# 16-head attention: ScalarE's blocks move from one PSUM ring to another

## The reference

```python
Q = (hs @ q_w + q_b).reshape(B, S, H, HD).transpose(0, 2, 1, 3)      # H = 16 heads
K = (hs @ k_w + k_b).reshape(B, S, H, KPH).transpose(0, 2, 1, 3)     # KPH = 4
V = (hs @ v_w + v_b).reshape(B, S, H, KPH).transpose(0, 2, 1, 3)
scores = einsum('bhsk,bhtk->bhst', Q[..., :KPH], K) / sqrt(KPH)
attn = softmax(scores, axis=-1)
ao = einsum('bhst,bhtv->bhsv', attn, V)       # 16 heads x 4 values, padded to 128
mla_out = ao @ o_w + o_b
```

## Time and profile before

| | |
|---|---|
| median of 3 runs | 1462.62 us (1462.22 to 1463.78) |
| the profiled execution | 1462.41 us |
| its span, which all positions below refer to | 1460.3 us |
| granted TensorE clock, mean | 0.943 of full speed |
| busy in the span: PE, VectorE, ScalarE, GpSimd | 1284.1, 1015.8, 931.7, 510.8 us |

### The profile page before, as it was taken

How to read it: one execution, slowest core, us unless ns; L and a number is a source line. 1 busy time by engine, 2 the same in 40 slices (tenths; PEclk the granted TensorE clock), 3 DMA queues, 4 the chain that set the end, 5 groups by cost and what they waited for, 6 DMA issues and landing times.

```text
span 1460.3 us, 17118 instructions
## 1 busy us (share of the span) xinstructions
PE 1284.1 (88%) x6134; PEld 693.6 (47%) x6134; DVE 1015.8 (70%) x1814; ACT 931.7 (64%) x1200; POOL 510.8 (35%) x358
## 2 busy tenths in 40 slices
PE   6999998999899999666878877899989999986666
PEld 3444453445344544331222222477756767763344
DVE  7788858885888578165776778356548676668895
ACT  4999978997899789432565666545545454433321
POOL 1445534553455344417433441023310000006333
PEclk9999999999999999866898999999999999998877
DMA  8100000000000000100000000000010000000000
GB/s 179 48 1 1 0 0 1 0 1 1 0 1 0 0 1 11 63 1 0 1 1 1 1 1 1 1 1 1 1 55 1 1 0 1 1 1 0 1 8 22
DMA packets 27711, 15.01 MB, mean 10 GB/s; under 512 B 16638, under 2 KB 26476, under 8 KB 27500
## 3 DMA queue, kind: packets, MB, share of 16 engines
q1 hardware_dynamic: 27628, 13.92, 3.6%
HBM read 12.86 MB, written 1.05 MB: 10 GB/s over the span
## 4 chain that ended last, share of the span: by engine, by line
PE 36%; issue 24%; POOL 21%; DVE 16%; ACT 2%; POOLq 0%; DMA 0%; SPq 0%; ACTq 0%; DVEq 0%
POOL ARENA L2145 10%; DVE ARENA L874 7%; POOL ARENA L2150 6%; PE PS L749 4%; PE PS L1066 4%; PE PS L732 4%; PE PS L608 3%; POOL ARENA L2157 3%; PE PS L650 3%; PE PS L1074 2%; PE PS L1097 2%; PE PS L617 2%; PE PS L1089 2%; PE PS L1078 2%; PE PS L1751 1%
## 5 line engine op out<-in xcount | busy, mean ns | idle before, releaser
L1751 PE MATMUL PS<-ARENA 128*128 128x512 f32 x512 | 227.3, 597 | 7.5 <-issue 6.7
L874 DVE TENSOR_REDUCE ARENA<-PS 128x1 f32<-128x512 f32 x256 | 160.1, 682 | 69.3 <-PE PS L617 69.1
L2042 DVE TENSOR_SCALAR ARENA<-PS,ARENA 128x512 f32<-128x512 f32 x256 | 188.1, 748 | 27.5 <-PE PS L1751 9.9
L2145 POOL TENSOR_TENSOR ARENA<-ARENA 128x1024 f32<-128x1024 f32 x64 | 151.5, 2367 | 131.6 <-ACT ARENA L1895 126.7
L794 ACT ACTIVATE ARENA<-PS 128x1024 f32<-128x1024 f32 x128 | 129.2, 1026 | 64.3 <-PE PS L636 64.0
L1751 PEld LDWEIGHTS PS<-ARENA 128*128 128x128 f32 x512 | 95.3, 191 | 117.3 <-issue 113.4
L1879 ACT ACTIVATE ARENA<-ARENA 128x2048 f32<-128x2048 f32 x64 | 119.7, 1905 | 47.6 <-DVE ARENA L2042 47.3
L1887 ACT ACTIVATE ARENA<-ARENA,consts_sb 128x2048 f32<-128x2048 f32 x64 | 127.8, 1996 | 0.4
L1760 PE MATMUL PS<-ARENA 128*64 128x512 f32 x512 | 119.9, 611 | 8.1 <-ACT ARENA L1895 8.1
L1895 ACT ACTIVATE ARENA<-ARENA 128x2048 f32<-128x2048 f32 x64 | 118.3, 1897 | 0.0
L617 PE MATMUL PS<-ARENA 32*128 32x512 bf16 x256 | 81.0, 402 | 39.7 <-DVE ARENA L874 27.9
(11 more groups left out here) (257 smaller groups left out, 2611.7 us busy)
## 6 DMA issues: line engine op xcount, KB each, us to landing
ARENA<-in_window_bias_dram SPq DMA_DIRECT2D x1, 1536.0 KB, 6.5
WKVG<-in_L_attn_W_in_dram SPq DMA_DIRECT2D x3, 448.0 KB, 6.7
X<-in_x_dram SPq DMA_DIRECT2D x4, 256.0 KB, 4.4
W<-in_L_ffn_w_dram SPq DMA_DIRECT2D x1, 1024.0 KB
out_dram<-X SPq DMA_DIRECT2D x4, 256.0 KB, 2.2
WQ<-in_L_attn_W_in_dram SPq DMA_DIRECT2D x2, 448.0 KB, 8.3
BV<-in_L_attn_b_in_dram SPq DMA_DIRECT2D x1, 512.0 KB, 6.8
Wout<-in_L_attn_W_out_dram SPq DMA_DIRECT2D x1, 512.0 KB, 4.8
```

The lines of the kernel that those rows point to most:

```text
L874: dve.tensor_reduce(NMX[:, w % 2, t, h:h + 1], bank(("cS", n, j)), AX.X, ALU.max, negate=True).then_inc(sem("c_max"), 1)
L1751: done(pe.matmul(o, SK[:, hd, kt * P:(kt + 1) * P], MQ[:, hd, :], start=True, stop=True), ("S", u, c))
L2042: dve.tensor_scalar(D[:, u % 2, hd, kt, :], bank(("S", u, c)), K2[:, u % 2, kt, hd:hd + 1], 1e-30, ALU.add, ALU.max).then_inc(sem("guarded ...
L2145: pool.tensor_tensor(WPAIR, D[:, u % 2, hd, 0:2], D[:, u % 2, hd, 2:4], ALU.add).then_inc(sem("w_paired"), 1)
```

## The change

The blocks that ScalarE reads leave the ring `cS` for `cP`: Q and K of a window become one two-bank block, and turned_out and project_out take one bank of `cP`. In `cS` stay the blocks that VectorE reads. TensorE signals once for Q and K together, so ScalarE's two activations both wait for both. In GpSimd's list the four additions `X + Y` move from between the first stacks to behind stacks 4 to 7.

```diff
--- before.py
+++ after.py
@@ -173,7 +173,7 @@
 
     def prepare(w):
         value = [(("cV", w // GROUPS), 1, [("c_v", w // GROUPS + 1)], "cS")] if w % GROUPS == 0 else []
-        return value + [(("cQ", w), 1, [("c_v32", 2 * w + 1)], "cS"), (("cK", w), 1, [("c_v32", 2 * w + 2)], "cS")]
+        return value + [(("cQK", w), 2, [("c_v32", 2 * w + 2)], "cP")]
 
     def maxima(n, j):
         return [(("cS", n, j), 1, [("c_max", 2 * n + j + 1)], "cS")]
@@ -195,9 +195,9 @@
         if at_window(n, 23) is not None:
             jobs += [(("cA", at_window(n, 23)), 1, [("c_ao", at_window(n, 23) + 1)], "cS")]
         if at_batch(n, 25) is not None:
-            jobs += [(("cT", at_batch(n, 25)), 1, [("c_aot", at_batch(n, 25) + 1)], "cS")]
+            jobs += [(("cT", at_batch(n, 25)), 1, [("c_aot", at_batch(n, 25) + 1)], "cP")]
         if at_batch(n, 27) is not None:
-            jobs += [(("cO", at_batch(n, 27)), 1, [("c_mla", at_batch(n, 27) + 1)], "cS")]
+            jobs += [(("cO", at_batch(n, 27)), 1, [("c_mla", at_batch(n, 27) + 1)], "cP")]
 
     jobs += [(("rt", 0), 1, [("r_logits", 1)])]
     jobs += [(("gt", i), 1, [("gram_turned", i + 1)]) for i in range(4)]
@@ -603,9 +603,10 @@
                         mm = pe.matmul(o[:, kt * 64:kt * 64 + 64], XT[:, b, kt * P:(kt + 1) * P], VW[:],
                                        start=True, stop=True)
                     done(mm, ("cV", b))
-                for side, key in enumerate(("cQ", "cK")):
-                    o = begin((key, w))
-                    done(pe.matmul(o, WX[:, side, g, :], XT[:, b], start=True, stop=True), (key, w))
+                o = begin(("cQK", w))
+                for side in range(2):
+                    mm = pe.matmul(o[:, side, :], WX[:, side, g, :], XT[:, b], start=True, stop=True)
+                done(mm, ("cQK", w))
 
             def maxima(n, j):
 
@@ -768,12 +769,12 @@
             def prepare(w):
 
                 g = w % GROUPS
-                for side, key in enumerate(("cQ", "cK")):
-                    full(act, (key, w))
-                    if w:
-                        act.wait_ge(sem("c_rest"), w)
+                full(act, ("cQK", w))
+                if w:
+                    act.wait_ge(sem("c_rest"), w)
+                for side in range(2):
                     c = side * GROUPS + g
-                    act.activation(V32[:, side], bank((key, w)), ACT.Identity,
+                    act.activation(V32[:, side], bank(("cQK", w))[:, side, :], ACT.Identity,
                                    bias=BQK[:, c:c + 1]).then_inc(sem("c_v32"), 1)
 
             def out_copy(w):
@@ -1009,13 +1010,12 @@
                 if w + 1 < WINS:
                     pool.wait_ge(sem("c_stack"), w + 1)
 
-            for b in range(B):
-                pool.wait_ge(sem("ln_y"), 2 * B + b + 1)
-                pool.tensor_tensor(X[:, b], X[:, b], Y[:, b], ALU.add).then_inc(sem("xy"), 1)
-                if b < 2:
-                    stack(b)
-            for w in range(2, WINS):
+            for w in range(WINS):
                 stack(w)
+                if 4 <= w < 4 + B:
+                    b = w - 4
+                    pool.wait_ge(sem("ln_y"), 2 * B + b + 1)
+                    pool.tensor_tensor(X[:, b], X[:, b], Y[:, b], ALU.add).then_inc(sem("xy"), 1)
             for i in range(B * NE):
                 b = i // NE
                 pool.wait_ge(sem("weighed"), i + 1)
```

## The result

The changed kernel took **1482.78 us** (median of 4 runs, 1480.71 to 1485.46), the kernel before in the same comparison 1463.2 us: a ratio of 1.013 with a 95% interval of 1.0105 to 1.0155. It is slower by 1.3%, clear of the interval, and outside the range of 1456.5 to 1469.0 us. The profiled execution took 1480.71 us, its span is 1478.6 us, 18.3 us longer than that of before.

The account below looks back on a forecast made before the run. It took each window as a loop of TensorE's S, projections and values, then VectorE's maxima and split, both counting in full. Gains and holds nearly cancelled, terms summing to +1.4 us: forecast 1464.0 us, range 1456.5 to 1469.0.

Parts of the forecast that it names:

- three signs: Casts keep 0.20 us, projections at 1.2 GHz differ from six by two or more, VectorE's S wait moves over 5 us.
- Q's and K's start: In ten ordinary windows, Q's matmuls no longer wait for add_maxima's bank, 0.11 us each: -1.1 us.
- batch windows: In two windows cV runs under ScalarE's copy of the turned output, so projections start sooner: -1.2 and -1.8, sum -3.0 us.
- project_out: Its bank no longer holds up the second S block behind it, 0.4 us in each of three batches: -1.2 us.
- last turned output: After it a P block, no longer an S block, waits for the copy: -0.3 us.
- The start of the stage: TensorE waits for the first stack, which comes 0.58 us later as both activations follow both projections: +0.6 us.
- Casts held by later stacks: Stacks ending 0.58 us later hold VectorE's split cast in six full-clock windows, 0.36 us each: +2.2 us.
- The cast that was caught already: The split cast at 696.89, already held by GpSimd's work, is held 0.6 us longer: +0.6 us.
- Additions: Behind stacks 4 to 7, each 1.24 us addition holds a cast of VectorE's split: +3.6 us in sum.
- Rival B: Held casts make more projections fall to 1.2 GHz, 1.6 us each; with three, 1468.8 us. Chance 0.25.
- Rival A: Clock stays up in two batch windows, -3.9 us; with VectorE held half as long as reckoned, 1457.2 us. Chance 0.25.
- Rival C: Nothing moves: ring waits were hidden, the 0.58 us disappears in ScalarE's waits, no cast is met: 1462.6 us. Chance 0.12.

Follow-up runs that it names:

- ring only: Kernel after, with the four additions back between the first stacks: 1475.36 us, ratio 1.0076.
- two signals with the longer split: Kernel after with a signal each for Q and K, additions in their old place, and VectorE's first split cast done three times: 1481.74 us, ratio 1.0122.
- one signal with side waits: Kernel after with additions in their old place, GpSimd's first two instructions of a stack each waiting for their own side: 1464.1 us, ratio 0.9961.
- before with the longer split: Kernel before, with VectorE's first cast of each split done three times instead of once: 1485.72 us, ratio 1.0148.
- two-signal kernel: Kernel after, with Q and K as two one-bank blocks in the same ring, each with its own signal: 1470.47 us, ratio 1.0036.
- Additions only: Kernel before, with only the four additions moved behind stacks 4 to 7: 1468.93 us, ratio 1.0042.
- the later stack: Kernel after with a signal each for Q and K, additions in their old place, one more GpSimd instruction heading each stack: 1473.74 us, ratio 1.0061.
- additions behind the split: Kernel after with a signal each for Q and K, each moved addition also waiting for its window's add_maxima: 1454.78 us, ratio 0.9939.
- After again: Kernel after, unchanged, timed once more on another chip: 1483.86 us, ratio 1.0115.
- two-signal kernel with the additions as before: Kernel after with a signal each for Q and K, and the additions back between the first stacks: 1454.57 us, ratio 0.9974.

## Why the prediction was wrong

**The step that failed.** The sum forecast +1.4 us, and +19.6 were measured. Taken together, its terms for rings, stacks and additions are not what was off. Its last sentence was: "What remains of the window is the same". TensorE's low time did not remain: it rose by 35.0 us in the loop and by 13.7 in the tail. Two of the three signs that the prediction gave for being wrong came true, eight projections at 1.2 GHz instead of six, and 7.3 us more of VectorE's wait.

**What the loop is made of.** Two kernels without a hold in an ordinary window, at 236.9 and 247.4 us, differ by 29.8 us of low time: 10.5 / 29.8 = 0.35 us of loop for each microsecond at 1.2 GHz. This price is fitted to two executions, and what follows is an account by it, not a proof. With it, and the excess lengths of the held instructions read from the timelines, the loops come out: ring only 236.9 + 0.35 x 37.9 + 2.6 = 252.8 (measured 253.0), after 236.9 + 0.35 x 50.5 + 5.8 = 260.4 (260.6), two signals with the longer split 236.9 + 0.35 x 41.8 + 7.2 = 258.7 (259.4). It misses others by 1 to 3 us (one signal with side waits 239.9 for 242.2, before with the longer split 3 too long). The executions of one kernel give a price too: a straight line of span over low time rises by 0.35 to 0.49 us per microsecond in the nine kernels with ten or more executions, but by only 0.21 to 0.26 in the kernel before. The Trainium skill, TensorE: Matmul & The Clock Gate, "Terms", puts the penalty at half of the time spent at the lower level. All these slopes lie below that half. An explanation that no run tests is that VectorE sets the pace of a part of the loop.

A difference of a few microseconds between two loops of the table shows no cause by itself. The five kernels with the new ring and no hold in an ordinary window have loops of 236.9 to 247.4 us and low times of 35.5 to 65.3 us. The 65.3 of them is above the 57.8 of the two-signal kernel, which has holds.

By this account the new ring is worth 249.3 - (236.9 + 0.35 x 15.5) = 7.0 us at the low time of before (15.5 is 51.0 less 35.5). For the change that is: -7.0 for the ring, +5.8 for holds, 0.35 x 35.0 = +12.3 for low time, together +11.1 of the 11.3 us measured. Point by point:

- **The ring's terms** (Q's and K's start, batch windows, project_out, last turned output, -5.6): 7.0 in all by the account, but not term by term. Q's and K's start gained next to nothing: at full clock Q starts 0.31 us behind the start of the S matmul ahead of it (822.40 to 822.71), 0.33 before, so -0.2 in ten windows and not -1.1. A whole ordinary window at full clock takes 14.47 us before (800.81 to 815.28) and in the two-signal kernel (793.54 to 808.01). The batch windows did gain: the one into which a batch's turned output falls takes 17.17 us before (815.28 to 832.45) and 15.86 in the two-signal kernel (808.01 to 823.87), both at full clock, -1.3 where the prediction had -1.2. (It took 832.62 for the start of those projections, and its own row has 832.45.) In the kernel after these windows ran low again, which is counted with the low time. Behind project_out VectorE waited 0.26 us at 845.04, below the 0.5 forecast.
- **The start of the stage** (+0.6): right. TensorE's wait for the first stack reads 7.02 us and not 5.78, but the first projections were shorter too, 4.75 us for 6.06. Additions only, whose first projections took 4.79 us, is the fair comparison: from their start to the first S block it is 11.18 us there and 11.78 in the kernel after.
- **Casts held by later stacks** (+2.2, six windows at 0.36): 0.34 each in five windows, +1.7. The mechanism, the place and the size of one were right. The cast that was caught already (+0.6) takes 0.69 us for 0.47, +0.2.
- **Additions** (+3.6): 4.1. The subtraction was held twice for 1.12 us longer and once for 0.93, the cast for 0.66 and 0.27. Stacks and additions together: forecast 5.8, measured 5.8.
- **The low time**: no term at all, where the account has +12.3 for 35.0 us. The forecast "gains and holds cancel" would have been near for the loop at an unchanged low time (-7.0 + 5.8).
- **Rival B** named this cause (held casts lengthen the stretch before the projections), and its direction was right, but it was undersized: it counted projections that fall. These went from six to eight of twelve, worth 3.2 us by its price; but the low stretches now cover S, P, values and cV too, as at 783 us. Its 1468.8 is 14 us short.
- **Rival A**'s mechanism works in the kernels with two signals, even with the later stack (1.98 us in both windows there), and not in the kernel after. **Rival C** fell: both ring and holds moved the time.
- **Left out altogether**: the tail and the stage behind it, +10.3 us in work that the change doesn't touch; and the 1.0 us that VectorE gains ahead of the stage, as the prediction had the additions cost nothing in their old place.

**What the 10.3 us are.** The executions of many of these kernels lie in two groups, or in three, as with the additions behind the split. *After again* ran at 1469.68 twice and at 1483.20 to 1486.23 eight times; the two-signal kernel with the additions as before at 1450.44 to 1454.94 six times and at 1461.97 to 1468.62 four times. The profile of *after again* fell in the lower group:

```profile
665.00:925.50 260.50, 213.31 (x1156) 60.63 (x1156) 191.63 (x406) 143.25 (x164) 109.88 (x95) 0.84 0.00 1
925.50:957.70 32.20, 27.01 (x200) 16.25 (x197) 10.82 (x45) 17.72 (x26) 0.00 (x0) 0.95 0.01 2
957.70:1089.00 131.30, 127.01 (x751) 94.15 (x749) 69.80 (x164) 68.31 (x102) 40.64 (x32) 0.99 0.03 10
1089.00:1321.00 232.00, 221.96 (x1343) 164.53 (x1344) 159.94 (x223) 111.07 (x398) 3.81 (x3) 0.99 0.01 5
1321.00:1467.00 146.00, 98.11 (x384) 61.68 (x382) 120.98 (x228) 41.41 (x76) 60.11 (x49) 0.82 0.03 8
```

Its loop is as long as after's (260.1 for 260.6), but tail (32.4 for 38.1), next stage (231.6 for 236.1) and rest (146.7 for 149.3) are 12.8 us shorter: the distance of the two groups. Tail and next stage come with a higher clock, but the rest's 2.6 us do not (0.82 in both). So about 10 of the 20 us are not in the edited stage but in which group an execution falls, and twelve of after's fourteen fall in the upper. That this share depends on the kernel is likely and not shown: the upper group has six of ten in ring only, four of ten with two signals, and the 17 executions of the three kernels with the extra GpSimd instruction or the longer split all lie in one group each, none 13 us below the rest. No run here shows what decides where TensorE's clock falls behind the loop. Nor is it shown why a delay of VectorE brings the low time that it brings, or why its amount varies as it does; that a delay brings it is shown by the longer split, with both rings. The longer time behind the loop, which the change met and no edit isolates, stays open.

## What to carry to other kernels

Where two engines work in a tight loop around each other, price a delay of one not only at its length but at what TensorE's clock makes of it: here 0.45 us per window, 7.2 us in all, cost 17 and 21 us. Before making a GpSimd instruction later, or moving one, look at the gap between its end and the next VectorE instruction on SBUF. Here gaps of 0.05 to 0.07 us closed when the stack came 0.58 us later, and a wait that places the addition beside VectorE's reading of PSUM cost nothing that could be measured. One trace of each kernel is little to go by where the clock moves: take the clock of every execution too. A signal that is merged to save a wait makes the earlier consumer later: let each consumer wait for its own part, which here was two waits instead of one in GpSimd's list.

## What the runs showed of the hardware

- A VectorE subtraction of 128x16 with two SBUF inputs was held for the whole of a GpSimd addition, 1.30 us instead of 0.18, as the casts are (1.27 for 0.20); row maxima from PSUM were not.
- The same hold falls on a longer chain: a layernorm step of 16 VectorE instructions took 5.11 us beside a GpSimd addition and 4.16 without it.
- TensorE's granted clock read 0.53 over 11 us in which the trace has it busy for 10.77; its instructions are longer there, as the projections show (3.78 us at the longest, 1.98 at full clock).
- One program has execution times 13 us apart on the same chip (1469.68 and 1483.20 us and more). Between the two profiled executions of it 10.2 of these us lie in two stretches in which the granted clock differs, 0.78 for 0.95 and 0.97 for 0.99. A median of a few executions of such a kernel says less than its ratio's narrow interval suggests.
